# Attention with PSUM as a ring of seven single banks and one bank for the weighted sums

## The chip, the cores and the metric

The kernel runs on one core of a Trainium2 chip. Its time is the device time in microseconds of one execution; three executions of the kernel before give a median of 1662.29 us.

## What is computed

A transformer block in four steps over x of shape (8, 512, 256), in float32: cross attention, a mixture of experts, cross attention again, and a linear layer with fp8 rounding. The change touches the two attentions. The first, cut to what matters:

```python
q = _split_heads(query @ wq.T + bq, B, S)      # 16 heads of 16
k = _split_heads(key @ wk.T + bk, B, S)
v = _split_heads(value @ wv.T + bv, B, S)
scores = jnp.einsum('bhqd,bhkd->bhqk', q, k) / math.sqrt(D_K)
p_attn = jax.nn.softmax(scores, axis=-1)
x = jnp.einsum('bhqk,bhkd->bhqd', p_attn, v)
```

The second does the same with other weights and no bias. Here B = 8, S = 512, H = 16.

## The kernel before

`build` runs nine stages one after the other; `attention(S, 0)` is the second and `attention(S, 1)` the seventh. The stages before each have left queries and keys in DRAM, with each number as two terms, and have taken the first 14 maxima (`AHEAD`).

A **group** is four heads of one batch entry: 32 groups (`NG`). A group has eight **units** (`UNITS`), i = 0 to 7, and a stage 256 units, s = 8n + i. The softmax subtracts the true maximum of a row, so each score is made twice: once as the **maximum pair** (`max_products`, L340), two matmuls of 64 rows by 512 columns for two heads, queries on the partitions, of which DVE takes the row maximum (L346), and once as the **score pair** (`score_unit`, L1062), keys on the partitions, in which the maximum is already subtracted as one more row of q. ACT takes the exponential of a score pair in one instruction over 1024 elements (L1120) into SBUF. The **weighted sum** (`values`, L1074) is four matmuls of 256 columns in float32 (eight in the profile, each as two passes), one for each head in a quarter of the array. Eight of them, numbered 0 to 7 here, make a group; number u needs the exponentials of units 0 to u, rounded up to an odd one. When all eight are done ACT copies the group's sums to SBUF (`take_outputs`, L1111), and SP stores them.

PSUM has eight banks of 512 float32. Six are the ring: three tensors of two banks (`ring`, L950), which maximum pairs and score pairs take in turn: maximum pair 0, score pair 0, maximum pair 1, score pair 1 and so on. The other two are `pout` (L951), one for the sums of even groups and one for those of odd groups.

The order on PE is written out by hand: a maximum pair, and then in every unit the score pair s, the maximum pair s + 1 and one weighted sum, the one of three units before (i >= 3: sum i - 3 of this group; i < 3: sum i + 5 of the group before). Score pair s waits for the maximum pair s - 1 to be reduced, since it takes its banks; maximum pair s + 1 waits for the exponential s - 1 (`exped`), whose banks it takes. The sum 0 of group n waits for the copy of group n - 2 (`taken`). After maximum pair 241 of the stage (`PAIRED` = 242) no maxima are left, and the last 14 units have a score pair and a sum only. ACT's order is the exponential of each unit, and behind that of unit 3 the copy of the group before. DVE reduces each maximum pair, and behind each eighth one turns the eight into rows of q (L1137, L1139, L1143), which SP moves to q. Before its first reduction it clears `pout` with two instructions (L1169), for which PE's first matmul waits (`clear`).

Of the kernel before, what the change touches and what calls it, by code (L numbers as in the profile page):

```python
# [21 lines left out]
G, HG = 4, 4  # L22
# [9 lines left out]
VW = DH + 1  # L32
# [248 lines left out]
UNITS = 2 * TPB  # L281
AHEAD = 2 * UNITS - 2
COLS = HG * TPB
ROUNDS_AHEAD = UNITS // 2 - 1
BLOCK = 32

class Inputs:
# [47 lines left out]
def max_products(e, bank, q, k, i):  # L336
    t, p = i // 2, i % 2
    for hh in range(2):
        at = slice(HALF * hh, HALF * (hh + 1))
        mm = e.matmul(bank[:, hh, :], q[at, p, t * P:(t + 1) * P], k[at, p, :], start=True, stop=True)  # L340
    return mm

def take_maxima(e, nmax, bank, i):
    t, p = i // 2, i % 2
    return e.tensor_reduce(nmax[:, :].rearrange("p (x y t) -> p x y t", x=2, y=2)[:, :, p, t], bank[:, :, :],  # L346
                           AX.X, ALU.max, negate=True)

def max_halves(nparts):  # L350
# [7 lines left out]
def move_maxima(e, q, nT, count):  # L358
    rows = q[MAX_ROWS[0]:MAX_ROWS[1], :, :].bitcast(F32).rearrange("s p (t i c) -> s (p t) i c", i=P // BLOCK, c=BLOCK)
    for i in range(P // BLOCK):  # L360
        e.dma_start(rows[:, :, i, :], nT[i * BLOCK:(i + 1) * BLOCK, :]).then_inc(count, 16)

class Ahead:
# [7 lines left out]
    def make(self, e, m):  # L372
        n = m // UNITS
        if m % UNITS == 0:
            e.wait_ge(self.inputs.ld[n], 16 * LOADS)
        if m >= 2:
            e.wait_ge(self.taken, m - 1)
        max_products(e, self.banks[m % 2], self.inputs.q[n], self.inputs.k[n], m % UNITS).then_inc(self.made, 1)
# [18 lines left out]
    def wait_moved(self, e):  # L397
        e.wait_ge(self.moved, 16 * (P // BLOCK))

# [534 lines left out]
def attention(S, l):  # L934
    nc = S.nc
    S.division = division = Division(S, l)
    ctx, sb, ps, sem = scope(S, f"a{l}")
    U = UNITS
    NG = B * G
    PAIRED = NG * U - AHEAD  # L940
    with ctx:
        inputs = S.inputs
        q = inputs.q + [sb(f"q{j}", [P, 2, SEQ], F32R) for j in range(EARLY_GROUPS, G)]
        k = inputs.k + [sb(f"k{j}", [P, 2, SEQ], F32R) for j in range(EARLY_GROUPS, G)]
        v = S.values.rows
# [12 lines left out]
        clear = sem("clear")  # L958
# [3 lines left out]
        maxed, reduced, cut, nturned = (sem(x) for x in ("maxed", "reduced", "cut", "nturned"))  # L962
        scored, exped, summed, taken = (sem(x) for x in ("scored", "exped", "summed", "taken"))
        oput = [sem(f"oput{j}") for j in range(2)]

        def max_bank(m):
            return ring[(AHEAD + 2 * (m - AHEAD)) % 3]

        def score_bank(s):
            return ring[(AHEAD + 1 + 2 * s if s < PAIRED else AHEAD + PAIRED + s) % 3]  # L970

        def spread_bank(b, kd):
            return score_bank(NG * U - 3 + b)[:, kd, :]

        def moved(n):
            return 16 * (P // BLOCK) * (n // G + (n % G > 0))

        def loaded(e, n):
            if n < G:
                e.wait_ge(ld_first[n], 16 * LOADS)  # L980
            else:
                e.wait_ge(ld[n % G], 16 * LOADS * (n // G))

        with nc.Block() as block:
# [63 lines left out]
            @block.tensor  # L1048
            def _(e):
                def max_unit(m):  # L1050
                    n, i = m // U, m % U
                    if i == 0:
                        loaded(e, n)
                    max_products(e, max_bank(m), q[n % G], k[n % G], i).then_inc(maxed, 1)

                def score_unit(n, i):
                    j, t, p = n % G, i // 2, i % 2
                    if i == 0 and n:
                        e.wait_ge(mrow[j], moved(n))
                    for hh in range(2):  # L1060
                        at = slice(HALF * hh, HALF * (hh + 1))
                        mm = e.matmul(score_bank(n * U + i)[:, hh, :], k[j][at, p, t * P:(t + 1) * P], q[j][at, p, :],  # L1062
                                      start=True, stop=True)
                    mm.then_inc(scored, 1)

                def values(n, t, half):
                    b, g = n // G, n % G
                    if t == 0 and half == 0:
                        if n >= 2:
                            e.wait_ge(taken, n - 1)  # L1070
                    e.wait_ge(exped, n * U + 2 * t + 2)
                    at = slice(half * D, (half + 1) * D)
                    for h in range(HG):
                        mm = e.matmul(pout[n % 2][32 * h:32 * h + VW, at], v[:, b * TPB + t, g * HG + h, :], pexp[t][:, h, at],  # L1074
                                      start=(t == 0 and half == 0), stop=(t == TPB - 1 and half == 1))
                    mm.then_inc(summed, 1)

                e.wait_ge(clear, 2)
                max_unit(AHEAD)
                for n in range(NG):  # L1080
                    for i in range(U):
                        s = n * U + i
                        if s < PAIRED:
                            if s:
                                e.wait_ge(reduced, s)
                        elif s == PAIRED + 1:
                            e.wait_ge(reduced, NG * U - AHEAD)
                        else:
                            e.wait_ge(exped, s - 1 if s == PAIRED else s - 2)
# [9 lines left out]
                for i in range(U - 3, U):  # L1099
                    values(NG - 1, i // 2, i % 2)  # L1100
                for b in range(SCALED_AHEAD):
                    for kd in range(KD):
                        division.spread_rows(e, spread_bank(b, kd), b, kd)

            @block.scalar
            def _(e):
                def take_outputs(n):
                    e.wait_ge(summed, (n + 1) * U)
                    if n >= 2:
                        e.wait_ge(oput[n % 2], 16 * (n // 2))  # L1110
                    e.activation(osb[n % 2][:, :], pout[n % 2][:, :], ACT.Copy).then_inc(taken, 1)  # L1111
# [12 lines left out]

            @block.vector
            def _(e):
                def reduce(m):
                    n = m // U
                    if m % U == 0 and n >= 3:
                        e.wait_ge(cut, 2 * (n - 2))  # L1130
                    e.wait_ge(maxed, m + 1 - AHEAD)
                    take_maxima(e, nmax[n % 2], max_bank(m), m % U).then_inc(reduced, 1)

                def turn_maxima(n):
                    halves, whole = max_halves(nparts[n % 2]), max_whole(nmax[n % 2])
# [1272 lines left out]
```

## Time and profile before

| | us |
|---|---|
| median of three executions | 1662.29 |
| lowest, highest | 1660.99, 1663.57 |
| span of the profiled execution | 1670.2 |
| first attention, paired phase | from 119.7 to 440 |
| second attention, paired phase | from 1226.1 to 1546 |

The durations below are those of the profiled execution, 7.9 us longer than the median. Its page shows the share of the span in which each engine was busy, and the same in 40 equal slices of 41.75 us: the first attention fills slices 3 to 11 (from 0), the second 29 to 37. A timeline row gives the start from the beginning of the span, the time from the first start to the last end of the instructions it merges, the engine, the line, and in brackets the idle time of the engine before it with what ended it. Matmuls are pipelined, so two rows of PE overlap; the distance of their starts is what tells the pace.

### The profile page before, as it was taken

What the parts mean: (1) busy time and instruction counts of PE and PEld (TensorE: products, weight loads), DVE (VectorE), ACT (ScalarE), POOL (GpSimd) and SP (SyncE); (2) the same over time, 40 slices, a digit from 0 to 9 for tenths busy, and PEclk for the clock granted to TensorE, in tenths of its full rate; (3) what the DMA queues carried; (4) which work ended last, traced back from release to release, by engine and by line L of the source; (5) the groups of instructions that cost most, each with busy time, mean ns of one, the idle gap of its engine ahead of it and who ended that gap; (6) DMA issues with size and microseconds to landing.
All of it is one profiled execution on the core that took longest, in us unless ns stands there. A gap on an engine that the chain in (4) does not pass through costs nothing. (4 is left out here: it accounts for less than half of the span.)

```text
span 1670.2 us, 28397 instructions
## 1 busy us (share of the span) xinstructions
PE 1513.5 (91%) x10910; PEld 979.2 (59%) x10910; DVE 1293.5 (77%) x2074; ACT 977.5 (59%) x1238; POOL 637.3 (38%) x957
## 2 busy tenths in 40 slices
PE   7989999999996289999999999779979999999846
PEld 6863333333385279999999999745523333333434
DVE  6789999999665856657665564379889999999787
ACT  5547888888833134444444444336548888888544
POOL 4314555555122135344342332255324444443120
PEclk9989999999996589999999999979979999999986
DMA  8974565555263022222223221168745555554103
GB/s 277 326 204 94 122 122 123 122 123 123 68 259 101 27 64 87 82 77 78 84 82 93 70 79 36 44 213 286 219 93 123 123 123 122 123 123 103 34 0 101
DMA packets 118742, 198.58 MB, mean 119 GB/s; under 512 B 29568, under 2 KB 63680, under 8 KB 117584
## 3 DMA queue, kind: packets, MB, share of 16 engines
q1 hardware_dynamic: 83840, 111.22, 21.9%
q0 software_dynamic: 33360, 83.94, 20.1%
q8 instruction: 87, 1.43, 0.4%
q10 hardware_dynamic: 1408, 1.61, 0.3%
q14 instruction: 47, 0.39, 0.1%
HBM read 117.77 MB, written 77.87 MB: 117 GB/s over the span
## 5 line engine op out<-in xcount | busy, mean ns | idle before, releaser
L1120 ACT ACTIVATE i_room<-a_ring 128x1024 f32<-128x1024 f32 x512 | 522.5, 1026 | 130.8 <-PE a_ring L1062 130.7
L346 DVE TENSOR_REDUCE logit<-a_ring 128x2 f32<-128x1024 f32 x484 | 576.9, 1220 | 26.7 <-PE a_ring L340 26.4
L1074 PE MATMUL a_pout<-i_room,values 128*17 128x256 f32 x4096 | 321.7, 387 | 0.7 <-ACT i_room L1120 0.7
L1755 ACT ACTIVATE e_full<-e_pH,b1T 128x320 f32<-128x320 f32 x256 | 135.0, 527 | 247.0 <-PE e_pH L1696 236.3
L1704 PE MATMUL e_pY<-fc_w,e_hid_hi 128*128 128x512 f32 x640 | 237.1, 407 | 0.6 <-DVE e_hid_lo L1808 0.6
L1062 PE MATMUL a_ring<-i_qk 64*128 64x512 f32 x768 | 194.9, 504 | 2.6 <-DVE logit L346 1.9
L1705 PE MATMUL e_pY<-fc_w,e_hid_lo 128*128 128x256 f32 x640 | 179.8, 281 | 0.0
L1062 PEld LDWEIGHTS a_ring<-i_qk 64*128 64x128 f32 x768 | 72.8, 186 | 169.7 <-DVE logit L346 103.1
L340 PE MATMUL a_ring<-i_qk 64*128 64x512 f32 x712 | 165.5, 461 | 6.0 <-DVE a_pout L1169 5.2
L1816 POOL DMA_INDIRECT w<-normed,slot_get x80 | 84.4, 1055 | 225.7 <-PE fc_turned L1681 199.6
L1808 DVE TENSOR_TENSOR e_hid_lo<-e_full,e_hid_hi 128x640 fp32r<-128x640 f32 x128 | 119.5, 934 | 55.7 <-ACT e_hid_hi L1764 55.7
L1696 PE MATMUL e_pH<-e_rowsT_hi,fc_w1T_hi 128*128 128x320 f32 x512 | 159.5, 312 | 0.0
L1696 PE MATMUL e_pH<-e_rowsT_lo,fc_w1T_hi 128*128 128x320 f32 x512 | 159.0, 311 | 0.0
L1696 PE MATMUL e_pH<-e_rowsT_hi,fc_w1T_lo 128*128 128x320 f32 x512 | 158.4, 309 | 0.0
L1074 PEld LDWEIGHTS a_pout<-i_room,values 128*17 128x17 f32 x4096 | 68.3, 95 | 129.7 <-issue 126.7
L1704 PEld LDWEIGHTS e_pY<-fc_w,e_hid_hi 128*128 128x128 f32 x640 | 120.3, 188 | 24.3 <-DVE e_hid_lo L1808 0.9
L1705 PEld LDWEIGHTS e_pY<-fc_w,e_hid_lo 128*128 128x128 f32 x640 | 121.3, 189 | 0.0
L1833 POOL DMA_INDIRECT ytok<-e_y,slot_put x80 | 82.7, 1034 | 93.0 <-DVE e_y L1788 78.3
L415 POOL DMA_DIRECT2D i_qk<-key_centre x42 | 24.1, 573 | 212.2 <-PE a_ring L1062 212.2
L1764 ACT ACTIVATE e_hid_hi<-e_full 128x640 fp32r<-128x640 f32 x128 | 94.6, 739 | 11.8 <-ACT e_full L1755 0.4
L1696 PEld LDWEIGHTS e_pH<-e_rowsT_hi,fc_w1T_hi 128*128 128x128 f32 x512 | 96.7, 189 | 5.6
L340 PEld LDWEIGHTS a_ring<-i_qk 64*128 64x128 f32 x712 | 67.9, 187 | 53.2 <-ACT i_room L1120 30.6
(334 smaller groups left out, 2530.2 us busy)
## 6 DMA issues: line engine op xcount, KB each, us to landing
ks<-i_room SPq DMA_DIRECT2D x64, 256.0 KB, 4.1
outs<-a_osb SPq DMA_DIRECT2D x64, 256.0 KB, 2.8
qs<-i_room SPq DMA_DIRECT2D x60, 256.0 KB, 4.7
fc_raw<-in_L_ffn_fc_w SPq DMA_DIRECT2D x15, 1024.0 KB, 5.4
i_qk<-ks POOLq DMA_DIRECT2D x84, 128.0 KB, 3.5
i_qk<-qs POOLq DMA_DIRECT2D x84, 128.0 KB, 3.6
BIG<-outs SPq DMA_DIRECT2D x64, 128.0 KB
ytok<-r_zeros SPq DMA_DIRECT2D x8, 1024.0 KB, 9.6
```

The source lines that it names most:

```text
L340: mm = e.matmul(bank[:, hh, :], q[at, p, t * P:(t + 1) * P], k[at, p, :], start=True, stop=True)
L346: return e.tensor_reduce(nmax[:, :].rearrange("p (x y t) -> p x y t", x=2, y=2)[:, :, p, t], bank[:, :, :], AX.X, ALU.max, negate=True)
L1062: mm = e.matmul(score_bank(n * U + i)[:, hh, :], k[j][at, p, t * P:(t + 1) * P], q[j][at, p, :], start=True, stop=True)
L1074: mm = e.matmul(pout[n % 2][32 * h:32 * h + VW, at], v[:, b * TPB + t, g * HG + h, :], pexp[t][:, h, at], start=(t == 0 and half == 0), st ...
L1120: e.activation(pexp[t][:, 2 * p:2 * p + 2, :], score_bank(n * U + i)[:, :, :], ACT.Exp).then_inc(exped, 1)
L1696: mm = e.matmul(pH[h][:, 0:WIDE], w1T[x][pl][:, k, f * P:(f + 1) * P], rowsT[j][pr][:, k, h * WIDE:(h + 1) * WIDE], start=(k == 0 and n_pa ...
L1704: e.matmul(pY[t][:, :, :], hid[s % 3][HI][:, token], w2[x][:, f, :, :], start=(f == 0), stop=False)
L1705: mm = e.matmul(pY[t][:, HI, :], hid[s % 3][LO][:, token], w2[x][:, f, HI, :], start=False, stop=(f == KF - 1))
L1755: e.activation(full[s % 2][:, h * WIDE:(h + 1) * WIDE], pH[h][:, 0:WIDE], ACT.Silu, bias=S.b1T[:, n * KF + f:n * KF + f + 1]).then_inc(act, 1)
L1764: e.activation(hid[s % 3][HI][:, :], full[s % 2][:, :], ACT.Copy).then_inc(hi, 1)
L1808: e.tensor_tensor(hid[s % 3][LO][:, :], full[s % 2][:, :], hid[s % 3][HI][:, :], ALU.subtract).then_inc(lo, 1)
L1816: e.indirect_dma_start(rows[:, t, :], None, S.normed[:, :], bass.IndirectOffsetOnAxis(ap=S.slot_get[:, c:c + 1], axis=0)).then_inc(ldr[0 i ...
```

## The change

The eight banks are divided anew. `ring` becomes one tensor of seven banks, and `pout` one bank. Maximum pairs and score pairs still take two banks each and in the same turn, but at any bank: use u of the ring begins at bank 2u mod 7 (`max_first`, `score_first`). Where it begins at bank 6, its second half is bank 0. There the exponential is two instructions, each with its own count of `exped`, and the reduction is two instructions (`take_maxima_apart`) with one count at the end; everywhere else both stay one instruction over two banks, and the exponential counts `exped` up by two. All waits on `exped` are rewritten in halves.

With one bank for the sums, those of group n can begin only when those of group n - 1 have been copied. So the last three sums of a group are made in units 0 and 1 of the next (one and two, `LATE_VALUES`), unit 2 has none, and ACT's copy stands behind the exponential of unit 1.

```diff
+BANKS = 7
+VALUE_LAG = 3
+LATE_VALUES = (UNITS - 3,), (UNITS - 2, UNITS - 1)
...
+def take_maxima_apart(e, nmax, banks, i):
+    t, p = i // 2, i % 2
+    for hh in range(2):
+        last = e.tensor_reduce(nmax[:, :].rearrange("p (x y t) -> p x y t", x=2, y=2)[:, hh, p, t:t + 1], banks[hh],
+                               AX.X, ALU.max, negate=True)
+    return last
...
-        ring = [ps(f"ring{j}", [P, 2, SEQ]) for j in range(3)]
-        pout = [ps(f"pout{j}", [P, SEQ]) for j in range(2)]
+        ring = ps("ring", [P, BANKS, SEQ])
+        pout = ps("pout", [P, SEQ])
...
-        def max_bank(m):
-            return ring[(AHEAD + 2 * (m - AHEAD)) % 3]
-
-        def score_bank(s):
-            return ring[(AHEAD + 1 + 2 * s if s < PAIRED else AHEAD + PAIRED + s) % 3]
+        def max_first(m):
+            return 4 * (m - AHEAD) % BANKS
...
+        def score_first(s):
+            use = 2 * s + 1 if s < PAIRED else PAIRED + s
+            return 2 * use % BANKS
...
                 def values(n, t, half):
                     b, g = n // G, n % G
-                    if t == 0 and half == 0:
-                        if n >= 2:
-                            e.wait_ge(taken, n - 1)
-                    e.wait_ge(exped, n * U + 2 * t + 2)
+                    if t == 0 and half == 0 and n:
+                        e.wait_ge(taken, n)
+                    e.wait_ge(exped, 2 * (n * U + 2 * t + 2))
...
                         if s < PAIRED:
                             if s:
                                 e.wait_ge(reduced, s)
+                            if s >= 2:
+                                e.wait_ge(exped, 2 * s - 2)
...
                         score_unit(n, i)
                         if s + 1 < PAIRED:
                             if s:
-                                e.wait_ge(exped, s)
+                                e.wait_ge(exped, 2 * s - 1)
                             max_unit(AHEAD + s + 1)
-                        if i >= 3:
-                            values(n, (i - 3) // 2, (i - 3) % 2)
-                        elif n:
-                            values(n - 1, (i + U - 3) // 2, (i + U - 3) % 2)
+                        if i >= VALUE_LAG:
+                            values(n, (i - VALUE_LAG) // 2, (i - VALUE_LAG) % 2)
+                        elif n and i < VALUE_LAG - 1:
+                            for v_unit in LATE_VALUES[i]:
+                                values(n - 1, v_unit // 2, v_unit % 2)
...
-                        e.activation(pexp[t][:, 2 * p:2 * p + 2, :], score_bank(n * U + i)[:, :, :], ACT.Exp).then_inc(exped, 1)
-                        if i == 3 and n:
+                        first = score_first(n * U + i)
+                        if first + 1 < BANKS:
+                            e.activation(pexp[t][:, 2 * p:2 * p + 2, :], ring[:, first:first + 2, :], ACT.Exp).then_inc(exped, 2)
+                        else:
+                            for hh in range(2):
+                                e.activation(pexp[t][:, 2 * p + hh, :], score_bank(n * U + i, hh), ACT.Exp).then_inc(exped, 1)
+                        if i == 1 and n:
                             take_outputs(n - 1)
...
-                for j in range(2):
-                    e.memset(pout[j][:, :], 0.0).then_inc(clear, 1)
+                e.memset(pout[:, :], 0.0).then_inc(clear, 1)
```

How it moves instructions, on PE first. The rows are units 2 and 3 of a group of the first attention, before the change; `a_ring<-i_qk` or `a_k,a_q` at L1062 is a score pair, at L340 a maximum pair, `a_pout` a weighted sum:

```order
L1062 MATMUL a_ring<-i_qk 128x512 [waits a0_reduced]
L1062 MATMUL a_ring<-i_qk 128x512
L340 MATMUL a_ring<-a_k,a_q 128x512 [waits a0_exped]
L340 MATMUL a_ring<-a_k,a_q 128x512
L1074 MATMUL a_pout<-i_room,values 17x256 [waits a0_exped]
L1074 MATMUL a_pout<-i_room,values 17x256 x3
L1062 MATMUL a_ring<-i_qk 128x512 [waits a0_reduced]
L1062 MATMUL a_ring<-i_qk 128x512
L340 MATMUL a_ring<-a_k,a_q 128x512 [waits a0_exped]
L340 MATMUL a_ring<-a_k,a_q 128x512
L1074 MATMUL a_pout<-i_room,values 17x256 [waits a0_exped,a0_taken]
L1074 MATMUL a_pout<-i_room,values 17x256 x3
```

The same place after the change, from the second weighted sum of unit 1 on (score pairs are L1080, maximum pairs L343, sums L1091):

```order
L1091 MATMUL a_pout<-i_room,values 17x256 [waits a0_exped]
L1091 MATMUL a_pout<-i_room,values 17x256 x3
L1080 MATMUL a_ring<-i_qk 128x512 [waits a0_exped,a0_reduced]
L1080 MATMUL a_ring<-i_qk 128x512
L343 MATMUL a_ring<-a_k,a_q 128x512 [waits a0_exped]
L343 MATMUL a_ring<-a_k,a_q 128x512
L1080 MATMUL a_ring<-i_qk 128x512 [waits a0_exped,a0_reduced]
L1080 MATMUL a_ring<-i_qk 128x512
L343 MATMUL a_ring<-a_k,a_q 128x512 [waits a0_exped]
L343 MATMUL a_ring<-a_k,a_q 128x512
L1091 MATMUL a_pout<-i_room,values 17x256 [waits a0_exped,a0_taken]
L1091 MATMUL a_pout<-i_room,values 17x256 x3
```

The sum of unit 2 has moved up into unit 1, two score pairs and two maximum pairs follow without a sum between them, and the wait on `taken` at unit 3 is now for the group just before.

On ACT, before, from the exponential of unit 1 on; L1111 is the copy:

```order
L1120 ACTIVATE i_room<-a_ring 128x1024 [waits a0_scored]
L1120 ACTIVATE i_room<-a_ring 128x1024 [waits a0_summed,a0_scored]
L1120 ACTIVATE i_room<-a_ring 128x1024 [waits a0_scored]
L1111 ACTIVATE a_osb<-a_pout 128x512 [waits a0_oput1,a0_summed]
L1120 ACTIVATE i_room<-a_ring 128x1024 [waits a0_summed,a0_scored]
```

After, from the exponential of unit 1 of a group whose unit 3 has banks 6 and 0; L1134 is the copy and L1148 an exponential over one bank:

```order
L1145 ACTIVATE i_room<-a_ring 128x1024 [waits a0_scored]
L1134 ACTIVATE a_osb<-a_pout 128x512 [waits a0_oput0,a0_summed]
L1145 ACTIVATE i_room<-a_ring 128x1024 [waits a0_summed,a0_scored]
L1148 ACTIVATE i_room<-a_ring 128x512 [waits a0_scored]
L1148 ACTIVATE i_room<-a_ring 128x512
L1145 ACTIVATE i_room<-a_ring 128x1024 [waits a0_summed,a0_scored]
```

The copy stands two exponentials earlier, and one exponential has become two instructions.

## Rows read from the trace of the kernel before

**Rows 1.** The page: busy time of each engine; TensorE's granted clock, in tenths, in 40 slices

```profile
PE 1513.5 (91%) x10910; PEld 979.2 (59%) x10910; DVE 1293.5 (77%) x2074; ACT 977.5 (59%) x1238; POOL 637.3 (38%) x957
...
PEclk9989999999996589999999999979979999999986
```

**Rows 2.** Waits, 128 to 440 us: engine, line, waited for, us, times, longest

```profile
ACT i_room L1120 <- PE a_ring L1062: 60.4, 208, 1.1
...
PEld a_ring L340 <- ACT i_room L1120: 20.3, 94, 0.2
DVE logit L346 <- PE a_ring L340: 12.0, 62, 0.9
```

**Rows 3.** Timeline of PE, one group of the first attention and its neighbour's start

```profile
301.33 0.62 PE L1074 MATMUL a_pout<-i_room,values 128*17 128x256 f32 x8
301.89 0.50 PE L1062 MATMUL a_ring<-i_qk 64*128 64x512 f32 x2
302.22 0.41 PE L340 MATMUL a_ring<-i_qk 64*128 64x512 f32 x2
302.56 0.63 PE L1074 MATMUL a_pout<-i_room,values 128*17 128x256 f32 x8
303.11 0.51 PE L1062 MATMUL a_ring<-i_qk 64*128 64x512 f32 x2
303.50 0.50 PE L340 MATMUL a_ring<-a_k,a_q 64*128 64x512 f32 x2
303.93 0.63 PE L1074 MATMUL a_pout<-i_room,values 128*17 128x256 f32 x8
304.49 0.50 PE L1062 MATMUL a_ring<-i_qk 64*128 64x512 f32 x2
...
305.81 0.50 PE L1062 MATMUL a_ring<-i_qk 64*128 64x512 f32 x2
...
307.09 0.50 PE L1062 MATMUL a_ring<-i_qk 64*128 64x512 f32 x2
...
312.41 0.50 PE L1062 MATMUL a_ring<-i_qk 64*128 64x512 f32 x2
```

**Rows 4.** The copies of 29 groups, first attention: ns min/median/max, first and last start

```profile
L1111 ACT ACTIVATE a_osb<-a_pout x29: 591/592/595, 138.8 to 434.0; 128x512 f32<-128x512 f32 x29
```

**Rows 5.** Timeline of ACT in the same group

```profile
302.43 1.02 ACT L1120 ACTIVATE i_room<-a_ring 128x1024 f32<-128x1024 f32 x1 [0.35 <-PE a_ring L1062]
303.65 1.02 ACT L1120 ACTIVATE i_room<-a_ring 128x1024 f32<-128x1024 f32 x1 [0.20 <-PE a_ring L1062]
...
307.27 0.59 ACT L1111 ACTIVATE a_osb<-a_pout 128x512 f32<-128x512 f32 x1
307.75 1.03 ACT L1120 ACTIVATE i_room<-a_ring 128x1024 f32<-128x1024 f32 x1
```

**Rows 6.** Timeline of DVE in the same group

```profile
303.93 0.18 DVE L1137 CAST logit<-logit 128x16 fp32r<-128x16 f32 x1
...
304.56 4.64 DVE L346 TENSOR_REDUCE logit<-a_ring 128x2 f32<-128x1024 f32 x4
```

**Rows 7.** Timeline of ACT behind the paired phase

```profile
443.80 0.59 ACT L1111 ACTIVATE a_osb<-a_pout 128x512 f32<-128x512 f32 x1
444.27 1.95 ACT L1120 ACTIVATE i_room<-a_ring 128x1024 f32<-128x1024 f32 x2
```

**Rows 8.** Timeline of PE at the stage's end, the last weighted sums

```profile
454.60 1.06 PE L1074 MATMUL a_pout<-i_room,values 128*17 128x256 f32 x16
456.00 1.06 PE L1074 MATMUL a_pout<-i_room,values 128*17 128x256 f32 x16 [0.34 <-ACT i_room L1120]
```

**Rows 9.** Timeline of ACT there, the last copy

```profile
457.12 0.60 ACT L1111 ACTIVATE a_osb<-a_pout 128x512 f32<-128x512 f32 x1 [1.18 <-PE a_pout L1074]
```

**Rows 10.** Timeline of DVE there, four operations over one bank each

```profile
457.75 2.48 DVE L918 TENSOR_TENSOR BIG<-BIG,a_ring 128x512 f32<-128x512 f32 x4 [11.46 <-PE a_ring L931]
```

**Rows 11.** Timeline of DVE at the start of the first attention, clearing `pout`

```profile
118.61 1.03 DVE L1169 MEMSET a_pout<- 128x512 f32 x2 [0.75 <-DVEq L547]
```

More of the change, by code:

```diff
@@ L333, in load_half, with max_products @@
             load_group(self.S, self.l, e, n, self.q[n], self.k[n], self.ld[n], range(half * (LOADS // 2), (half + 1) * (LOADS // 2)))
-def max_products(e, bank, q, k, i):
+def max_products(e, banks, q, k, i):
     t, p = i // 2, i % 2
@@ L339, in max_products, with take_maxima @@
         at = slice(HALF * hh, HALF * (hh + 1))
-        mm = e.matmul(bank[:, hh, :], q[at, p, t * P:(t + 1) * P], k[at, p, :], start=True, stop=True)
+        mm = e.matmul(banks[hh], q[at, p, t * P:(t + 1) * P], k[at, p, :], start=True, stop=True)
     return mm
-def take_maxima(e, nmax, bank, i):
+def take_maxima(e, nmax, pair, i):
     t, p = i // 2, i % 2
-    return e.tensor_reduce(nmax[:, :].rearrange("p (x y t) -> p x y t", x=2, y=2)[:, :, p, t], bank[:, :, :],
+    return e.tensor_reduce(nmax[:, :].rearrange("p (x y t) -> p x y t", x=2, y=2)[:, :, p, t], pair[:, :, :],
                            AX.X, ALU.max, negate=True)
+def take_maxima_apart(e, nmax, banks, i):
[4 more added lines that the diff above has]
+    return last
 def max_halves(nparts):
@@ L377, in make @@
             e.wait_ge(self.taken, m - 1)
-        max_products(e, self.banks[m % 2], self.inputs.q[n], self.inputs.k[n], m % UNITS).then_inc(self.made, 1)
+        max_products(e, [self.banks[m % 2][:, hh, :] for hh in range(2)], self.inputs.q[n], self.inputs.k[n], m % UNITS).then_inc(self.made, 1)
     def take(self, e, m):
@@ L964, in attention, with max_banks, score_bank @@
         oput = [sem(f"oput{j}") for j in range(2)]
-        def max_bank(m):
-            return ring[(AHEAD + 2 * (m - AHEAD)) % 3]
-        def score_bank(s):
-            return ring[(AHEAD + 1 + 2 * s if s < PAIRED else AHEAD + PAIRED + s) % 3]
+        def max_first(m):
+            return 4 * (m - AHEAD) % BANKS
+        def max_banks(m):
+            return [ring[:, (max_first(m) + hh) % BANKS, :] for hh in range(2)]
+        def score_first(s):
+            use = 2 * s + 1 if s < PAIRED else PAIRED + s
+            return 2 * use % BANKS
+        def score_bank(s, hh):
+            return ring[:, (score_first(s) + hh) % BANKS, :]
         def spread_bank(b, kd):
-            return score_bank(NG * U - 3 + b)[:, kd, :]
+            return ring[:, b * KD + kd, :]
         def moved(n):
@@ L1085, in _ @@
                                 e.wait_ge(reduced, s)
+                            if s >= 2:
+                                e.wait_ge(exped, 2 * s - 2)
+                        elif s == PAIRED:
+                            e.wait_ge(exped, 2 * s - 3)
                         elif s == PAIRED + 1:
-                            e.wait_ge(reduced, NG * U - AHEAD)
+                            e.wait_ge(reduced, PAIRED)
+                            e.wait_ge(exped, 2 * s - 4)
                         else:
-                            e.wait_ge(exped, s - 1 if s == PAIRED else s - 2)
+                            e.wait_ge(exped, 2 * s - 5)
                         score_unit(n, i)
@@ L1092, in _ @@
                             if s:
-                                e.wait_ge(exped, s)
+                                e.wait_ge(exped, 2 * s - 1)
                             max_unit(AHEAD + s + 1)
-                        if i >= 3:
-                            values(n, (i - 3) // 2, (i - 3) % 2)
-                        elif n:
-                            values(n - 1, (i + U - 3) // 2, (i + U - 3) % 2)
-                for i in range(U - 3, U):
+                        if i >= VALUE_LAG:
[3 more added lines that the diff above has]
+                                values(n - 1, v_unit // 2, v_unit % 2)
+                for i in range(U - VALUE_LAG, U):
                     values(NG - 1, i // 2, i % 2)
@@ L1110, in take_outputs @@
                         e.wait_ge(oput[n % 2], 16 * (n // 2))
-                    e.activation(osb[n % 2][:, :], pout[n % 2][:, :], ACT.Copy).then_inc(taken, 1)
+                    e.activation(osb[n % 2][:, :], pout[:, :], ACT.Copy).then_inc(taken, 1)
                 inputs.wait_stored(e)
@@ L1131, in reduce @@
                     e.wait_ge(maxed, m + 1 - AHEAD)
-                    take_maxima(e, nmax[n % 2], max_bank(m), m % U).then_inc(reduced, 1)
+                    first = max_first(m)
+                    if first + 1 < BANKS:
+                        take_maxima(e, nmax[n % 2], ring[:, first:first + 2, :], m % U).then_inc(reduced, 1)
+                    else:
+                        take_maxima_apart(e, nmax[n % 2], max_banks(m), m % U).then_inc(reduced, 1)
                 def turn_maxima(n):
```

8 lines of the change are left out of this document (4 added, 4 removed).

## Prediction, made before the changed kernel was run

> **What bounds the kernel now.** The change touches the two attention stages alone. Each is a run of 256 units; for the first 242 of them (the paired phase) PE makes in every unit one score pair, one maximum pair and one weighted sum. I read first the busy shares: PE is busy nearly all of the time and the clock is granted in full there, and DVE and ACT are far from idle [rows 1]. Such shares don't tell who waits for whom, so next the waits of the paired phase of the first attention [rows 2]: PE's maximum pair waits 94 times for the exponential, ACT's exponential waits 208 times for a score pair, and DVE waits little. Last, one group of eight units in order of time. The group that begins with the score pair at 301.89 takes 10.52 us to the next at 312.41 [rows 3], and 28 groups take 295.2 us, 10.54 each [rows 4].
>
> Within it I name units by i = 0 to 7 and read four prices. A maximum pair that doesn't wait starts 0.33 after its score pair (301.89, 302.22), the weighted sum 0.34 later (302.56), the next score pair 0.55 after that (303.11): a **free** unit of 1.22. In the next unit the maximum pair starts 0.39 after the score pair, the sum 0.43 later, the next score 0.56 later: a **held** unit of 1.38 (303.11 to 304.49) [rows 3]. What holds it is the exponential of the unit before: it starts 0.54 after its score pair (302.43 for 301.89), lasts 1.02, and the maximum pair starts 0.05 after its end (303.50) [rows 3, 5]. So score i, exponential i, maximum pair of unit i+1, sum, score i+2 is a loop of 0.54 + 1.02 + 0.05 + 0.99 = 2.60 us for two units. A free unit is always followed by a held one, and after a held one the next is free: four times 2.60 is 10.40, and the rest to 10.52 is the copy of the weighted sums, which stands between exponentials 3 and 4 and makes the latter start 0.66 instead of 0.54 after its score (307.75 for 307.09) [rows 3, 5]. This loop through PE and ACT sets the pace, and DVE fits into it: after its small steps at 303.93 it has four maxima waiting, takes them in 4.64 us [rows 6] and has time left to wait for PE, 62 times in the phase [rows 2].
>
> **The change part by part. The ring.** Seven banks in place of six look like half a pair more. But an exponential over neighbouring banks counts up its semaphore by two at its end, so the maximum pair of unit i+1 still waits for the whole of exponential i. Only where the pair is banks 6 and 0 (s = 1 mod 7, 35 of 242, and 2 more behind them) is the exponential two instructions, and its first half frees what the maximum pair needs. The trace of before has no exponential over one bank. The nearest row is the copy, as wide and also from PSUM: 0.59 long, and the next instruction of ACT starts 0.48 after it [rows 7]. So the halves start 0.48 apart, the first ends at 0.59 and the second at 1.07, in place of 1.02: the free slots of ACT before its exponentials (0.35 and 0.20 in this group, 60.4 us over the phase [rows 2, 5]) hide the 0.05.
>
> **The weighted sums in one bank.** All late sums of group n-1 must be done before the copy, and the copy before the first sum of group n at i = 3. So unit 1 now makes two sums, unit 2 none, and the copy stands behind exponential 1. Step by step, for a group without a split exponential:
> - Unit 0, free: 1.22.
> - Unit 1, held, with a second sum. Sixteen matmuls of the sum take 1.06 [rows 8] where eight take 0.62 [rows 3]: 0.44 more. 1.38 + 0.44 = 1.82.
> - Units 2 and 3. The sixteen end 1.06 after their start and score 2 starts 1.00 after it; the copy starts 0.06 after their end, as at 457.12 [rows 8, 9], so 0.12 after score 2. Exponential 2 is queued behind it on ACT and starts 0.59 after score 2 (0.12 + 0.48, rounded), 0.05 later than it would. It ends at 1.62, and maximum pair 3 starts at 1.67. PE wanted to make it far earlier: unit 2 has no sum, so score 3 could start some 0.67 after score 2. It waits for DVE until 0.88 (before, score 3 starts 3.92 after score 0, just behind the first of the four maxima [rows 3, 6]; 3.92 - 1.22 - 1.82 = 0.88), and maximum pair 3 could start at 1.21. It is held 0.46 us. Then 0.99 to score 4: 2.66 for both units.
> - Units 4 to 7: free, held, free, held, 2 x 2.60 = 5.20.
> Sum 1.22 + 1.82 + 2.66 + 5.20 = 10.90, so **0.38 more than 10.52**. In words: the second sum of unit 1 costs 0.44, the empty place in unit 2 gives nothing back, since the loop of 2.60 runs from score 2 to score 4 whatever PE has in between, and the copy's place gives 0.1 back.
>
> **What the split exponentials give back.** Over seven groups each i has one. At i = 2 the first half ends at 0.59 + 0.59, so maximum pair 3 starts at 1.23 and score 4 some 0.45 earlier. At i = 0, 4 and 6 a held unit becomes free, 0.15 each. At odd i the next maximum pair wasn't held. (0.45 + 0.45) / 7 = 0.13 per group. Net 0.25 per group, 29 groups with a full paired phase in each of two stages: **+14.5 us**. The bounds of this term: no relief, 58 x 0.38 = +22.0; twice the relief, 58 x 0.12 = +7.0.
>
> A rule speaks to this. The Trainium skill, Perfetto Trace Analysis, section Optimizing Scalar/DVE Operations, says that where ScalarE or VectorE isn't saturated but causes bubbles elsewhere, breaking up its instructions may let work finish sooner. By it every one of the eight splits helps, 0.45 + 7 x 0.15 = 1.5 in seven groups, and the term would be 58 x (0.38 - 0.21) = +9.9 in place of +14.5. The free and held units of the trace speak for four of the eight, and that is what I take.
>
> **Maxima.** 34 of 242 per stage become two reductions. No row has one over a single bank. Bounds: nothing, and the nearest DVE rows of 512 elements, four in 2.48 us [rows 10], some 0.60 apart (2.48 = 3 x 0.60 + 0.68), against 1.14 for a whole one of 1024 (4.64 = 3 x 1.14 + 1.22) [rows 6]: 0.06 more for each pair of halves, 4 us for all 68 if they stood in the way. DVE gets through its queue after each turn and then waits, and score 3, the only one it holds, has 0.46 to spare now. I take 0.
>
> **Start and end.** One memset less: PE begins behind two that take 1.03 [rows 11], so up to 0.52 per stage; I take -1.0 for both, the bound is 0. In the 14 units behind the paired phase the same burst and gap stand on PE; ACT is nearly as loaded there, I take 0, within 0.5 per stage. Other waits (SP's store of the outputs comes two units earlier, GpSimd's loads wait for scores as before) have slack.
>
> Sum: +14.5 - 1.0 = **+13.5 us**. The profiled execution is 1670.2, 7.9 above the median of 1662.29; the profile would give 1684 and the median **1676**.
>
> **Rivals.**
> - Slower by the whole price (0.15): the split halves bring no relief, because PE takes the free unit back in the next held one, or the two reductions stop the score behind them. 1662.3 + 22.0 - 1.0 = 1683, with the maxima's 4 up to 1687.
> - No difference (0.12): the relief outweighs what I counted: each split shifts the pattern so that two held units become free. It needs 0.38 x 7 = 2.7 us in seven groups, three times mine. 1659 to 1665.
> - Faster (0.10): the second sum costs nothing. Four held units lose 0.16 each, 0.64 a group, more than the 0.44 of the burst; were PE's order loose enough to fill them, the group would be 10.52 - 0.12 - 0.13 = 10.27, and the time 1662 - 58 x 0.25 - 1 = 1647. It decides at maximum pair 3: only if it starts by 1.21 after score 2 is the burst paid back. Exponential 2 needs until 1.62, so the trace speaks against it. The same page of the Trainium skill (Optimization Strategy) says that consistent bubbles can mean too little PSUM for the next tile; by that rule a seventh bank would lift the held units. Here it does so only where an exponential is split.
>
> **How the numbers follow.** Forecast 0.63 (1668 to 1681). With 0.15 above and 0.22 below, the range of 8 in 10 is 1665 to 1686. A measurement can tell about 0.2%, 3.3 us. Faster by more 0.10; within 0.12; slower 0.78.
>
> **What would show it.** In the profile after: groups of 10.9 us, with some of about 10.75 and one in seven near 10.5; score 1 to score 2 about 1.8; maximum pair 3 waiting for ACT by 0.4 to 0.5; the copy right after score 2 starts; halves 0.48 apart. I am wrong if maximum pair 3 isn't held, if the halves take as long as a whole one, or if score pairs wait longer for DVE.

## The result, and the profile after

| | before | after |
|---|---|---|
| median, us | 1662.57 (4 executions) | 1691.32 (4 executions) |
| lowest, highest | 1660.99, 1663.57 | 1688.76, 1692.10 |
| ratio, 95% interval | | 1.0175 (1.0161 to 1.0190) |

The change makes the kernel 28.8 us slower. The forecast was slower by 13.5 us, to 1676: the right sign, less than half the size, and a time outside the range, whose upper end was 1686.

First the page of the changed kernel, its length and its busy times. Against [rows 1] PE is 5 us less busy, ACT 7 us and DVE 11 us more, so no engine has gained work that would make 20 us. The program has 790 instructions more (28397 before):

```profile
span 1689.8 us, 29187 instructions
PE 1508.9 (89%) x10910; PEld 973.0 (58%) x10910; DVE 1304.4 (77%) x2140; ACT 984.8 (58%) x1312; POOL 636.1 (38%) x957
```

Then the waits of the same stretch as [rows 2], 128 to 440 us. The maximum pair's wait for the exponential has grown from 20.3 to 32.0 us and its longest from 0.2 to 0.7 us, and DVE's wait for the maximum pair is about as it was:

```profile
PEld a_ring L343 <- ACT i_room L1145: 32.0, 98, 0.7
DVE logit L349 <- PE a_ring L343: 12.7, 58, 0.8
```

The copies of the groups, one line as [rows 4]: 317.2 us for 29 groups, 10.94 each, where it was 10.54.

```profile
L1134 ACT ACTIVATE a_osb<-a_pout x30: 597/598/600, 135.7 to 452.9; 128x512 f32<-128x512 f32 x30
```

One group in order of time, as [rows 3]. L1080 is the score pair, L343 the maximum pair, L1091 the weighted sum; unit 0 begins at 296.73, unit 1 at 297.95, unit 2 at 299.82, unit 3 at 300.65, unit 4 at 302.51:

```profile
296.73 0.50 PE L1080 MATMUL a_ring<-i_qk 64*128 64x512 f32 x2
...
297.95 0.50 PE L1080 MATMUL a_ring<-i_qk 64*128 64x512 f32 x2
298.40 0.50 PE L343 MATMUL a_ring<-i_qk 64*128 64x512 f32 x2
298.83 1.06 PE L1091 MATMUL a_pout<-i_room,values 128*17 128x256 f32 x16
299.82 0.50 PE L1080 MATMUL a_ring<-i_qk 64*128 64x512 f32 x2
300.16 0.39 PE L343 MATMUL a_ring<-i_qk 64*128 64x512 f32 x2
300.65 0.49 PE L1080 MATMUL a_ring<-i_qk 64*128 64x512 f32 x2
301.52 0.50 PE L343 MATMUL a_ring<-i_qk 64*128 64x512 f32 x2 [0.38 <-ACT i_room L1145]
301.95 0.63 PE L1091 MATMUL a_pout<-i_room,values 128*17 128x256 f32 x8
302.51 0.49 PE L1080 MATMUL a_ring<-i_qk 64*128 64x512 f32 x2
```

And ACT in it, as [rows 5]; L1134 is the copy:

```profile
297.32 1.02 ACT L1145 ACTIVATE i_room<-a_ring 128x1024 f32<-128x1024 f32 x1 [0.38 <-issue]
298.56 1.02 ACT L1145 ACTIVATE i_room<-a_ring 128x1024 f32<-128x1024 f32 x1 [0.21 <-PE a_ring L1080]
299.96 0.60 ACT L1134 ACTIVATE a_osb<-a_pout 128x512 f32<-128x512 f32 x1 [0.38 <-PE a_pout L1091]
300.45 1.94 ACT L1145 ACTIVATE i_room<-a_ring 128x1024 f32<-128x1024 f32 x2
```

The **burst**, as the two sums in unit 1 are called below, goes as foretold: its sixteen matmuls take 1.06 us, score 2 comes 1.87 us after score 1, the copy starts 0.14 and exponential 2 0.63 after score 2, and maximum pair 3, which could start 0.33 after score 3, at 300.98, starts at 301.52, held by 0.54. What is not as foretold stands in units 0 and 1. Exponential 0 starts 0.59 after its score pair (297.32 for 296.73), exponential 1 0.61 after (298.56 for 297.95); before it was 0.54. So maximum pair 1 starts 0.45 after score 1 and not 0.39.

For the two attention stages, from the start of their first ring matmul to the start of their last score pair, the trace has 346.6 and 346.8 us; experiment E8 below has 334.0 and 334.1 for the kernel before. That is 25.3 of the 27.9 us between these two spans.

### The profile page after: what moved, and what is told of

The parts are those of the page before. It is cut to its first block and busy times, and to the rows that moved or that the text cites. A ratio compares the mean times of both kernels' runs of the same rounds, so it can differ in the third digit from the quotient of the medians.

```text
span 1689.8 us, 29187 instructions
## 1 busy us (share of the span) xinstructions
PE 1508.9 (89%) x10910; PEld 973.0 (58%) x10910; DVE 1304.4 (77%) x2140; ACT 984.8 (58%) x1312; POOL 636.1 (38%) x957
## 5 line engine op out<-in xcount | busy, mean ns | idle before, releaser
L349 DVE TENSOR_REDUCE logit<-a_ring 128x2 f32<-128x1024 f32 x416 | 503.7, 1221 | 34.8 <-PE a_ring L343 28.2
L1145 ACT ACTIVATE i_room<-a_ring 128x1024 f32<-128x1024 f32 x438 | 445.3, 1030 | 115.8 <-PE a_ring L1080 95.4
L1091 PE MATMUL a_pout<-i_room,values 128*17 128x256 f32 x4096 | 310.0, 386 | 1.7 <-ACT i_room L1145 1.1
L1080 PE MATMUL a_ring<-i_qk 64*128 64x512 f32 x768 | 194.1, 503 | 12.4 <-DVE logit L349 8.6
L1080 PEld LDWEIGHTS a_ring<-i_qk 64*128 64x128 f32 x768 | 72.7, 186 | 176.5 <-issue 84.3
L343 PE MATMUL a_ring<-i_qk 64*128 64x512 f32 x712 | 161.5, 450 | 13.3 <-ACT i_room L1145 8.5
L1091 PEld LDWEIGHTS a_pout<-i_room,values 128*17 128x17 f32 x4096 | 74.7, 95 | 138.9 <-issue 107.9
L343 PEld LDWEIGHTS a_ring<-i_qk 64*128 64x128 f32 x712 | 68.4, 189 | 61.2 <-ACT i_room L1145 49.5
```

The costliest lines, as they stand in the source:

```text
L343: mm = e.matmul(banks[hh], q[at, p, t * P:(t + 1) * P], k[at, p, :], start=True, stop=True)
L1080: mm = e.matmul(score_bank(n * U + i, hh), k[j][at, p, t * P:(t + 1) * P], q[j][at, p, :], start=True, stop=True)
L1091: mm = e.matmul(pout[32 * h:32 * h + VW, at], v[:, b * TPB + t, g * HG + h, :], pexp[t][:, h, at], start=(t == 0 and half == 0), stop=(t = ...
L1145: e.activation(pexp[t][:, 2 * p:2 * p + 2, :], ring[:, first:first + 2, :], ACT.Exp).then_inc(exped, 2)
```

## Experiments

Each experiment states its edit against the kernel before or the changed one. The times are medians of executions; those of before, run beside them, had medians of 1662.09 (E1 to E4) and 1663.58 (E5 to E8). A ratio and its interval are worked out over all executions, so a ratio can differ a little from the quotient of two medians. Beside the copies, the distance from one group's first score pair to the next one's is given as the length of a group, over the 56 groups 2 to 29 of both stages; it differs from that of the copies by about 0.01.

### E1: the changed kernel, an exponential counts by one

```diff
+        def exped_before(s):
+            return sum(1 if score_first(r) + 1 < BANKS else 2 for r in range(s))
...
-    e.wait_ge(exped, 2 * s - 1)
+    e.wait_ge(exped, exped_half(s - 1))
...
-    e.activation(..., ring[:, first:first + 2, :], ACT.Exp).then_inc(exped, 2)
+    e.activation(..., ring[:, first:first + 2, :], ACT.Exp).then_inc(exped, 1)
```

> The changed kernel, but an exponential over two banks counts its semaphore up by one, as one over a single bank does; all waits on it are rewritten for that, nothing else moves. Theory A (in the profile after, an exponential that counts by two starts 0.59 to 0.60 us after its score pair, one that counts by one 0.54, because its wait has become an instruction of its own on ACT): every exponential starts 0.54 after its score, held units fall from 1.44 to 1.38, a group from 10.94 to about 10.77, the time from 1691 by 10 to about 1681. Rival B (the missing 15 us come from the second wait on PE's score pairs, or from the maxima that are two reductions): both are still there, groups stay at 10.94, the time at 1689 to 1693.

Measured: 1679.86 us, ratio 1.0103 (1.0084 to 1.0122), 11.5 us less than the changed kernel. The page's first line, ACT's exponentials of units 0 and 1 in the group whose score pairs start at 289.26 and 290.48, and the copies (10.80 us a group):

```profile
span 1676.9 us, 28961 instructions
```
```profile
289.80 1.03 ACT L1154 ACTIVATE i_room<-a_ring 128x1024 f32<-128x1024 f32 x1 [0.31 <-PE a_ring L1089]
291.02 1.02 ACT L1154 ACTIVATE i_room<-a_ring 128x1024 f32<-128x1024 f32 x1 [0.20 <-PE a_ring L1089]
```
```profile
L1143 ACT ACTIVATE a_osb<-a_pout x30: 597/598/600, 130.2 to 443.3; 128x512 f32<-128x512 f32 x30
```

Theory A holds, rival B falls: the 68 double reductions and the second wait on PE's score pairs are still in this kernel, and its groups are within 0.04 of the 10.77 that were forecast without them.

This run also shows group by group what a split exponential gives. The 24 groups that have one at odd i only take 10.94 us on the mean, as long as those of E3 below, which has none. The 24 with one at i = 0, 4 or 6 take 10.77, and the 8 with one at i = 2 take 10.53. In one of those eight, whose score 2 is at 335.70, maximum pair 3 starts 1.27 after score 2 and score 4 at 2.26:

```profile
336.33 1.08 ACT L1157 ACTIVATE i_room<-a_ring 128x512 f32<-128x512 f32 x2
```
```profile
336.97 0.50 PE L343 MATMUL a_ring<-i_qk 64*128 64x512 f32 x2
337.96 0.50 PE L1089 MATMUL a_ring<-i_qk 64*128 64x512 f32 x2
```

### E2: the kernel before, each exponential counts by two

```diff
-    e.wait_ge(exped, s)
+    e.wait_ge(exped, 2 * s)
...
-    e.activation(pexp[t][:, 2 * p:2 * p + 2, :], score_bank(n * U + i)[:, :, :], ACT.Exp).then_inc(exped, 1)
+    e.activation(pexp[t][:, 2 * p:2 * p + 2, :], score_bank(n * U + i)[:, :, :], ACT.Exp).then_inc(exped, 2)
```

> The kernel before, but each exponential counts by two and every wait on it is doubled; nothing else. Theory A: each exponential starts 0.05 to 0.06 later after its score pair, the loop of two units grows from 2.60 to 2.66 us, a group from 10.54 to 10.76, the time from 1662 by some 13 to about 1675. Rival B: the step of the count costs nothing, 1660 to 1665.

Measured: 1677.20 us, ratio 1.0081 (1.0062 to 1.0099). The copies are 10.70 us apart (299.5 for 28), 0.16 more than in [rows 4], and the page counts 264 instructions more than for the kernel before, all on ACT in the raw record. The exponential at 268.80 belongs to the score pair at 268.21, 0.59 before it:

```profile
span 1675.5 us, 28661 instructions
```
```profile
268.21 0.49 PE L1062 MATMUL a_ring<-i_qk 64*128 64x512 f32 x2
```
```profile
268.80 1.02 ACT L1120 ACTIVATE i_room<-a_ring 128x1024 f32<-128x1024 f32 x1 [0.35 <-PE a_ring L1062]
```
```profile
L1111 ACT ACTIVATE a_osb<-a_pout x29: 591/592/594, 134.8 to 434.3; 128x512 f32<-128x512 f32 x29
```

Rival B falls: the step of a count costs 15 us by the medians, 13.5 by the ratio, in a kernel in which nothing else has changed. Per group it is 0.16 and not the expected 0.22: exponential 4, which stands behind the copy, starts 0.65 after its score here and 0.64 in E8, so units 4 and 5 together grow by 0.01 and the other three pairs of units by 0.05 to 0.06 each. The groups make 9 us of the difference; where the other 4 to 6 lie isn't shown.

### E3: the kernel before, only the weighted sums in one bank

```diff
-    e.wait_ge(taken, n - 1)          # n >= 2
+    e.wait_ge(taken, n)              # n >= 1
...
-    mm = e.matmul(pout[n % 2][32 * h:32 * h + VW, at], ...
+    mm = e.matmul(pout[0][32 * h:32 * h + VW, at], ...
...
-    elif n:
-        values(n - 1, (i + U - 3) // 2, (i + U - 3) % 2)
+    elif n and i < 2:
+        for v_unit in ((U - 3,), (U - 2, U - 1))[i]:
+            values(n - 1, v_unit // 2, v_unit % 2)
...
-    if i == 3 and n:
+    if i == 1 and n:
         take_outputs(n - 1)
```

> The kernel before with its ring of three pairs and its count by one; only the weighted sums change: one bank for all groups, the last three sums in units 0 and 1 of the next group (one and two), none in unit 2, ACT's copy behind the exponential of unit 1. Theory A (as predicted): maximum pair 3 is held by 0.4 to 0.5 us, a group takes 10.90 (0.38 more), the time rises by 22 to about 1684. Rival C (the burst fits into PE's slack and the ring of seven banks is what costs): 1660 to 1666.

Measured: 1687.92 us, ratio 1.0139 (1.0117 to 1.0162): 25.8 us more than before by the medians, 23 by the ratio. The copies are 10.93 apart, where 10.90 had been worked out. The steps of the prediction can be read off one group, whose score 2 is at 285.21: copy 0.14 after it, exponential 2 at 0.63, score 3 at 0.88, maximum pair 3 at 1.71, score 4 at 2.69.

```profile
285.21 0.50 PE L1062 MATMUL a_ring<-a_q,a_k 64*128 64x512 f32 x2
285.55 0.40 PE L340 MATMUL a_ring<-i_qk 64*128 64x512 f32 x2
286.09 0.50 PE L1062 MATMUL a_ring<-a_q,a_k 64*128 64x512 f32 x2
286.92 0.50 PE L340 MATMUL a_ring<-i_qk 64*128 64x512 f32 x2 [0.32 <-ACT i_room L1120]
287.35 0.63 PE L1073 MATMUL a_pout<-i_room,values 128*17 128x256 f32 x8
287.90 0.50 PE L1062 MATMUL a_ring<-a_q,a_k 64*128 64x512 f32 x2
```
```profile
285.35 0.60 ACT L1111 ACTIVATE a_osb<-a_pout 128x512 f32<-128x512 f32 x1 [0.38 <-PE a_pout L1073]
285.84 1.94 ACT L1120 ACTIVATE i_room<-a_ring 128x1024 f32<-128x1024 f32 x2
```
```profile
L1111 ACT ACTIVATE a_osb<-a_pout x30: 597/597/598, 132.2 to 449.1; 128x512 f32<-128x512 f32 x30
```

Rival C falls: with the ring of three pairs untouched, the sums in one bank cost the whole price. From E3 to E1 a group is 0.13 shorter, the relief that was worked out for the one split exponential in seven. The two kernels differ in the ring, the split reductions and PE's second wait as well; that the gain belongs to the splits is shown by the groups of E1, which are shorter only where a split stands at an even i.

### E4: ring of seven, count by one, one sum in every unit

```diff
-LATE_VALUES = (UNITS - 3,), (UNITS - 2, UNITS - 1)
+LATE_VALUES = (UNITS - 3,), (UNITS - 2,), (UNITS - 1,)
...
-    if i == 1 and n:
+    if i == 2 and n:
         take_outputs(n - 1)
```

on top of E1.

> The ring of seven banks with the count by one, and the weighted sums as before the change, one in every unit: the last three in units 0, 1 and 2, the copy behind the exponential of unit 2, and the first sum of the next group, in unit 3, waits for the copy. Theory A (the burst with the empty place is the cost, one bank for the sums is not): the copy runs until 0.7 us after score pair 3, the first sum waits for it by 0.1 at most, groups take 10.3 to 10.5, the time is 1650 to 1662. Rival D (one bank for the sums costs by itself, since PE now waits for ACT's copy in each group and ACT's next exponential stands behind it): groups of 10.8 or more, 1675 to 1690.

Measured: 1662.72 us, ratio 0.9997 (0.9984 to 1.0010), and groups of 10.51 (294.2 us for 28), both just outside what theory A gave:

```profile
L1143 ACT ACTIVATE a_osb<-a_pout x29: 591/597/606, 131.8 to 426.0; 128x512 f32<-128x512 f32 x29
```

Rival D falls. Without the burst a group is 0.30 shorter than in E1, and the time 17 us. Against the kernel before a group is only 0.03 shorter, and its units tell why. Units 4 and 5 take 2.60 and not 2.72 us, since the copy no longer stands ahead of exponential 4. Units 2 and 3 take 2.71 and not 2.61: there the first sum waits for the copy. The other four take 2.60 a pair as before, so the split exponentials, which gave 0.13 a group in E1, give nothing that can be seen here; why is not shown. Behind the paired phase the last 14 score pairs take 13.8 us in the kernel before and 15.2 here, 1.4 more in each stage, since there too the first sum waits for the copy and PE's next score pair stands behind it. So one bank for the sums costs 0.1 a group and 1.4 a stage, and moving the copy gives about as much back.

### E5 to E7: every exponential in halves

E5 is the changed kernel with all exponentials in two instructions, and E4's order of the sums; E7 is the same with the changed kernel's order, two sums in unit 1 and none in unit 2. Edit of both:

```diff
-    first = score_first(n * U + i)
-    if first + 1 < BANKS:
-        e.activation(pexp[t][:, 2 * p:2 * p + 2, :], ring[:, first:first + 2, :], ACT.Exp).then_inc(exped, 2)
-    else:
-        for hh in range(2):
-            e.activation(pexp[t][:, 2 * p + hh, :], score_bank(n * U + i, hh), ACT.Exp).then_inc(exped, 1)
+    for hh in range(2):
+        e.activation(pexp[t][:, 2 * p + hh, :], score_bank(n * U + i, hh), ACT.Exp).then_inc(exped, 1)
```

E6 does it to the kernel before, whose ring is three pairs; the maximum pair's two matmuls wait for one half each:

```diff
+    for hh in range(2):
+        if halves:
+            e.wait_ge(exped, halves - 1 + hh)
+        mm = e.matmul(max_bank(m)[:, hh, :], ...
```

> Ring of seven banks, every exponential two instructions of one bank with a count of one each, sums one in every unit (copy behind the exponential of unit 2). Theory A (the pace is set by the loop score, exponential, maximum pair; a first half frees the bank that the next maximum pair needs): no maximum pair is held, units take 1.22 us, score 3 waits 0.25 for DVE behind its turn and the first sum 0.1 for the copy, a group takes 10.1 to 10.3, the time is 1635 to 1650. Rival E (ACT's fixed cost per instruction, twice as often, makes ACT or PE's many waits the bound, as grouping into one instruction was meant to save): groups of 10.5 or more, 1660 to 1680.

> The kernel before (three pairs, two banks for the sums), every exponential two instructions with a count of one each; the first matmul of a maximum pair waits for the first half, the second for the second half. Theory A: the second half ends 1.07 us after the exponential's start, later than the whole one's 1.02, and in a ring of pairs the maximum pair needs it: its second matmul is held as before or by 0.05 more, groups of 10.5 to 10.75, 1660 to 1675. Rival F (it is the splitting that helps, the seventh bank has no part in it): groups near 10.2, 1640 to 1650.

> The changed kernel with its two sums in unit 1 and none in unit 2, but every exponential two instructions of one bank. Theory A (the burst costs because maximum pair 3 must wait for a whole exponential 2): the first half ends about 1.2 us after score 2, just when maximum pair 3 could start, so the empty place in unit 2 pays the burst back; groups of 10.1 to 10.3, 1638 to 1650, as without the burst. Rival G (two sums in one unit cost their 0.44 us whatever ACT does): groups of 10.5 to 10.7, 1660 to 1675.

| | median, us | ratio, 95% interval | group, us |
|---|---|---|---|
| E5 | 1640.47 | 0.9861 (0.9846 to 0.9876) | 10.08 |
| E6 | 1676.72 | 1.0080 (1.0066 to 1.0094) | 10.71 |
| E7 | 1639.20 | 0.9856 (0.9841 to 0.9871) | 10.08 |

The copies of E6, from which its 10.71 is taken (289.1 us for 27):

```profile
L1116 ACT ACTIVATE a_osb<-a_pout x28: 605/606/609, 135.7 to 424.8; 128x512 f32<-128x512 f32 x28
```

E5 and E7 beat both kernels, by 23 to 24 us against the one before and by 51 to 52 against the changed one. The timeline of PE in E7, units 0 to 4 of a group (score pairs at 280.56, 281.77, 283.42, 284.54, 285.75), with the copy and the halves on ACT:

```profile
281.77 0.50 PE L1080 MATMUL a_ring<-i_qk 64*128 64x512 f32 x2
282.11 0.40 PE L343 MATMUL a_ring<-i_qk 64*128 64x512 f32 x2
282.44 1.06 PE L1091 MATMUL a_pout<-i_room,values 128*17 128x256 f32 x16
283.42 0.50 PE L1080 MATMUL a_ring<-i_qk 64*128 64x512 f32 x2
283.76 0.40 PE L343 MATMUL a_ring<-i_qk 64*128 64x512 f32 x2
284.54 0.50 PE L1080 MATMUL a_ring<-i_qk 64*128 64x512 f32 x2 [0.38 <-DVE logit L349]
284.87 0.40 PE L343 MATMUL a_ring<-i_qk 64*128 64x512 f32 x2
```
```profile
283.56 0.60 ACT L1134 ACTIVATE a_osb<-a_pout 128x512 f32<-128x512 f32 x1 [0.16 <-PE a_pout L1091]
284.06 3.32 ACT L1144 ACTIVATE i_room<-a_ring 128x512 f32<-128x512 f32 x6
```
```profile
L1134 ACT ACTIVATE a_osb<-a_pout x30: 597/597/598, 132.2 to 424.6; 128x512 f32<-128x512 f32 x30
```

No maximum pair is held: over units 16 to 239 of both stages none starts more than 0.34 after its score, in E5 nor in E7, while in E8 169 of 448 do. Maximum pair 3 starts at 284.87, 1.45 after score 2, where E3 had 1.71, and what it waits behind is score 3, which waits for DVE. So the burst is paid back by the empty place in unit 2, and E7 is as fast as E5: rivals E and G fall. The price of the burst was the wait for the whole exponential 2, and not the work of PE. What limits the pace now is DVE: it is busy for 293.7 of the 300 us from 130 to 430 (285.1 in the kernel before), while PE, busy for 299.6 us in the kernel before, is busy for 288.7. The row gives the busy times of PE, its weight loads, DVE, ACT and GpSimd:

```profile
130.00:430.00 300.00, 288.69 (x2864) 106.51 (x2859) 293.72 (x360) 271.91 (x509) 165.15 (x287) 1.00 0.53 122
```

In E6 the unit that waits shows what the pairs cost. Its maximum pair (L1059) starts 0.34 after the score pair, but takes 0.61 and not 0.40, and PE's weight loads tell why: the second stands 0.35 behind the first, released by ACT.

```profile
270.72 0.50 PE L1069 MATMUL a_ring<-i_qk 64*128 64x512 f32 x2
271.06 0.61 PE L1059 MATMUL a_ring<-i_qk 64*128 64x512 f32 x2
```
```profile
270.83 0.19 PEld L1059 LDWEIGHTS a_ring<-i_qk 64*128 64x128 f32 x1
271.18 0.18 PEld L1059 LDWEIGHTS a_ring<-i_qk 64*128 64x128 f32 x1 [0.16 <-ACT i_room L1126]
```

In a ring of pairs the second matmul needs the second half, which ends 1.09 after the start of the first, where a whole exponential ends after 1.02. Rival F falls: halves alone make the kernel before 13 us slower, and only with the seventh bank, which moves the pairs against each other by one bank, do they gain. E6's time is 2 us above the range that was given for it; its groups are in theirs.

### E8: the kernel before once more

> The kernel before once more, for its profile: the profiled execution shown first is 8 us above the median of its kind. If its attention stages are as long as there (334.5 us each from first to last ring matmul), the 8 us lie in other stages and the attention stages of the two kernels differ by 24 us; if they are shorter by 2 us each, the whole of the measured 29 us lies in them.

Measured: a span of 1661.9 us, groups of 10.55, attention stages of 334.0 and 334.1 us. The span of the first profile is 8.3 us longer, and of these 0.9 lie in the two attention stages (334.5 us each there); the first ring matmul is at 116.0 us here and at 119.7 there. So neither of the two cases of the expectation is met exactly: against E8 the stages of the two kernels differ by 25.3 us.

## Why the prediction was right and wrong

- **What sets the pace**: right. E5 and E7 take away the loop's whole exponential and with it every held unit. The pattern was simpler than the trace, though: in E8 score 3 waits for DVE, units 2 and 3 take 1.31 and 1.30 us, and no more than 169 of 448 maximum pairs are held. The pairs of units take 2.61 all the same, and the one behind the copy 2.72.
- **The burst**: right, with 10.90 worked out and 10.93 measured in E3, 23 us in 58 groups. Taken out of the ring of seven (E1 to E4) it gives 0.30 a group back, 17 us; the two are not the same edit, since E4 makes the first sum wait for the copy.
- **The relief of the split exponentials**: right from E3 to E1, both in size (0.13 per group) and in place: a split at i = 2 shortens a group by 0.41 where 0.45 was worked out, one at 0, 4 or 6 by 0.17 (0.15), and one at odd i by nothing. The changed kernel has the same order, with groups of 10.66, 10.90 and 11.09. It doesn't carry over to E4, where it is gone.
- **"An exponential over neighbouring banks counts up its semaphore by two at its end"**: this is the step that failed. It was used for what it releases and given no price, so the term stood at 0 without a reason. The exponential starts 0.05 to 0.06 later after its score pair, and since it stands in the loop of two units this lengthens the loop. From E1 to the changed kernel a group grows by 0.14, 8 us in 58 groups, and the median by 11.5. With these 8 us the forecast would have been 1684, inside its range and still 7 below the measured time. The trace of before has no exponential that counts by two and so could not price it.
- **Start**: -1.0 was taken. The first ring matmul starts 0.53 after the one clearing instruction, where it was 1.08 after the first of two, so 0.5 per stage is there; it lies ahead of the stages as they are measured here. Behind it the first group, which has no burst yet, takes 13.7 and 13.9 us in the two stages, against 12.6 and 13.0 in E8. This goes with the clock rather than with the edit: TensorE's granted clock over the first 13 us of the stages is 0.56 on the mean in the changed kernel's profile and 0.64 in E8. In the first profile of before, the same kernel as E8, it is 0.58 and 0.60 and the first group takes 13.2 and 13.4; in E1 it is 0.65 and 0.58 for 12.6 and 13.6.
- **End**: 0 within 0.5 was taken. The last 14 score pairs take 13.6 us and not 13.8.
- **Maxima**: 0 was taken. The reductions over one bank last 0.69 and 0.68 and end 1.29 after the start, 0.07 later than a whole one; the groups of E1 with splits at odd i, as long as those of E3, leave nothing for them.

Between the profile of the changed kernel and E8 the 25.3 us of the two stages divide as follows: 23.0 in the 56 groups 2 to 29, 0.6 in the second group, 2.1 in the first, and -0.4 at the end. The 23.0 are reached in steps: 22.5 from E8 to E3, -7.5 from E3 to E1, 8.0 from E1 to the changed kernel. For all 58 groups the forecast had 14.5, and of the 9 us that it lacks, 8 are the count. The medians differ by 28.8; the 3.5 us beyond the 25.3 stay open. In the profiles 2.4 us lie ahead of the first attention, where nothing was edited; E1's profile reaches it 4.6 us earlier than that of the changed kernel with the same code.

By the Trainium skill (Perfetto Trace Analysis, section Optimizing Scalar/DVE Operations), breaking up instructions of an engine that isn't saturated but holds others up may let work finish sooner. The prediction worked out 0.21 a group for the case that each of the eight splits in seven groups helps; the groups of E1 show 0.13, and nothing for a split at odd i. Done for every exponential, with the count by one, it gives 0.72 us a group against E1 (10.81 to 10.09); in the ring of pairs (E6) it gives a loss. The rival that spoke of a seventh bank lifting the held units was wrong for this change, and right as soon as the instruction that frees the bank covers one bank only.

## What to carry to other kernels

A ring of single banks is only as fine as the instruction that empties it: if the reader covers two banks and reports once, the odd bank brings nothing that shows (10.51 against 10.54 us a group in E4), and here its price was the second bank for the sums. Before a burst is moved into slack, follow the loop that makes the slack: the burst was paid almost in full (0.39 of 0.44 us a group in E3) while the loop waited for a whole exponential, and was free when the loop waited for half of one (E7 against E5). A count by two in place of one is an edit with a price where it stands on the loop (0.14 us a group here, 0.16 in E2).
